# Where the pad rows of the expert queues are read from: 16 partitions with eight rows each, in place of 128 with one

## The reference

```
x = layernorm(x + dilated_attention(x))              # 16 heads, segments of 64, every second token
x = layernorm(x + cross_attention(x, ctx, ...))      # 16 heads, causal, context of 64 channels
x = layernorm(x + moe(x))                            # 32 experts, 8 for each token
```

## Time and profile before

| | us |
|---|---|
| median of three runs | 625.43 |
| lowest, highest | 625.3, 627.13 |
| span of the profiled execution | 719.4 |
| first half, until the last pad has landed (from the chain of waits) | 380.93 |
| first load of a block issued | 381.23 |
| TensorE's first work on a block | 383.46 |

### The profile page before, as it was taken

One profiled execution on the slowest core, in us unless ns is written; L12 is line 12 of the kernel. 1 busy time (PEld: TensorE's weight loads), 2 busy tenths in 40 slices (PEclk: granted clock), 3 DMA queues, 4 the chain that ended last, 5 costly groups with the idle time before them and its releaser, 6 DMA issues.

```text
span 719.4 us, 17476 instructions
## 1 busy us (share of the span) xinstructions
PE 563.9 (78%) x5097; PEld 414.4 (58%) x5098; DVE 368.4 (51%) x1527; ACT 330.1 (46%) x1204; POOL 390.5 (54%) x599
## 2 busy tenths in 40 slices
PE   3768787888878888888306889988998888985995
PEld 2445454544555554444105777777777776774884
DVE  1537566666677566666402444444444444443453
ACT  2445555455455455456003555555555554553012
POOL 5443445545544455545551666766666666665432
PEclk9789999999999899999556999999999999998899
DMA  9999996111111111112285554555555454554994
GB/s 206 277 275 365 342 339 231 69 59 73 68 50 64 55 73 73 65 66 74 99 308 182 155 165 150 160 156 167 152 164 159 143 157 142 164 160 148 425 418 145
DMA packets 83069, 121.31 MB, mean 169 GB/s; under 512 B 13779, under 2 KB 72669, under 8 KB 80992
## 3 DMA queue, kind: packets, MB, share of 16 engines
q1 hardware_dynamic: 64128, 78.46, 36.3%
q0 software_dynamic: 14016, 38.44, 14.7%
q10 hardware_dynamic: 4896, 4.03, 1.7%
HBM read 56.07 MB, written 69.01 MB: 174 GB/s over the span
## 4 chain that ended last, share of the span: by engine, by line
PE 54%; issue 12%; ACT 12%; DVE 9%; DMA 6%; ACTq 3%; POOL 2%; SPq 1%; another core or an unknown queue 0%; DVEq 0%; POOLq 0%
PE bank L793 14%; PE bank L809 9%; ACT pr L870 7%; PE bank L611 5%; PE bank L785 5%; PE bank L601 4%; PE bank L803 3%; PE bank L661 3%; DMA out<-fin 3%; PE bank L744 2%; DMA wall<-results 2%; DVE nmax L1024 2%; PE bank L619 2%; ACTq L296 1%; DVE tg L1218 1%
## 5 line engine op out<-in xcount | busy, mean ns | idle before, releaser
L556 POOL DMA_INDIRECT results<-ys,wcol x152 | 150.1, 988 | 25.8 <-POOL pscrap L545 22.0
L530 POOL DMA_INDIRECT queues<-x,xidx x128 | 129.1, 1009 | 36.9 <-issue 36.5
L793 PE MATMUL bank<-wall,xtT 128*128 x616 | 127.1, 330 | 0.7 <-issue 0.7
L870 ACT ACTIVATE pr<-bank,nmax 128x128 f32<-128x128 f32 x256 | 90.9, 370 | 29.1 <-DVE nmax L1024 29.1
L1218 DVE SCALAR_TENSOR_TENSOR tg<-th,bank 128x96 f32<-128x96 f32 x154 | 39.1, 254 | 125.3 <-ACT th L957 96.9
L793 PEld LDWEIGHTS bank<-wall,xtT 128*128 128x128 f32 x616 | 98.4, 194 | 1.4 <-issue 1.3
L963 ACT ACTIVATE ys<-bank,wcol 128x256 f32<-128x256 f32 x152 | 71.9, 473 | 54.6 <-PE bank L809 36.6
L809 PE MATMUL bank<-wall,hT 96*128 x304 | 94.5, 392 | 0.0
L785 PE MATMUL bank<-ident,xt 128*128 128x128 f32 x310 | 63.3, 286 | 35.4 <-DMA xt<-queues 24.1
L785 PEld LDWEIGHTS bank<-ident,xt 128*128 128x128 f32 x310 | 59.0, 197 | 49.9 <-DMA xt<-queues 25.1
L876 ACT COPY prT<-bank 128x512 f32<-128x512 f32 x64 | 38.5, 601 | 88.9 <-PE bank L611 86.2
(11 more groups left out here) (178 smaller groups left out, 947.2 us busy)
## 6 DMA issues: line engine op xcount, KB each, us to landing
xt<-queues SPq DMA_DIRECT2D x162, 160.0 KB
results<-zeros SPq DMA_DIRECT2D x16, 1024.0 KB
wall<-results SPq DMA_DIRECT2D x16, 1024.0 KB, 12.7
queues<-zeros SPq DMA_DIRECT2D x32, 160.0 KB, 4.9
wall<-in_L_ffn_w_gate SPq DMA_DIRECT2D x4, 768.0 KB
wall<-in_L_ffn_w_up SPq DMA_DIRECT2D x4, 768.0 KB
wall<-in_L_ffn_w_down SPq DMA_DIRECT2D x4, 768.0 KB
results<-ys,wcol POOLq DMA_INDIRECT x152
```

The costliest lines, as they stand in the source:

```text
L530: pool.indirect_dma_start(xg, bass.IndirectOffsetOnAxis(ap=xidx[:, par, k:k + 1], axis=0), x2[:, par, :], None, bounds_check=last_row, oob ...
L556: pool.indirect_dma_start(yr, bass.IndirectOffsetOnAxis(ap=wcol[:, u, 1:2], axis=0), ys[:, u, :], None, bounds_check=last_y, oob_is_err=Fa ...
L793: ins = pe.matmul(bank[2 + u % 2][:, 0:2 * INTER].rearrange("p (g i) -> p g i", g=2), xtT[:, u % 2, kk, :], wall[:, bass.ds(e, GU)].rearrange(
L870: ins = act.activation(pr[:, g % 2, q, :], pS[g % 2][:, q * P:(q + 1) * P], ACT.Exp, bias=nmax[:, 4 * g + q:4 * g + q + 1], accum_out=den[ ...
```

## The change

The pad's source is no longer `zeros` but the first 16 partitions of `xt`. GpSimd fills their eight slots with the pad row (two more memsets behind those of `zeros`), so that each of the 16 partitions holds eight pad rows one behind the other, 10,240 bytes. A pad's DMA then has 16 rows of 2560 words on both sides. Bytes, number and issuers of the pads are the same, and `zeros` stays for the idle blocks and for clearing `results`.

```diff
+PADP = P // UN
...
-N_CONST = 49
+N_CONST = 51
...
                 for r in rows:
-                    eng.dma_start(xg[bass.ds(r, P), :], zeros[:, :]).then_inc(signal, 16)
+                    eng.dma_start(xg[bass.ds(r, P), :].rearrange("(p k) w -> p (k w)", k=UN),
+                                  xt[0:PADP, :, :].rearrange("p k w -> p (k w)")).then_inc(signal, 16)
...
             def late_constants():
                 put(pool.memset, zeros[:, 0:D + NE], 0.0)
                 put(pool.memset, zeros[:, D + NE:XW].bitcast(I32), int(FAR))
+                put(pool.memset, xt[0:PADP, :, 0:D + NE], 0.0)
+                put(pool.memset, xt[0:PADP, :, D + NE:XW].bitcast(I32), int(FAR))
                 put(pool.memset, onesb[:, :], 1.0)
```

## The result

The changed kernel takes 659.71 us, the median of four runs (659.31 to 661.66), against 625.63 us for the kernel before on the same chip (625.3 to 627.13). The ratio is 1.0551, with a 95% interval of 1.0519 to 1.0583: slower by 34.1 us. The forecast was 655.5 us, range 645 to 674.

A forecast was written before the change was run, and what follows sets the result against it. Full DMA engines moving pads and scatters between the halves were taken as the bound: 49.0 us of pads plus 2.3 of scatters, 51.3 in place of 21.2, +30.1 on 625.4, gives 655.5 us, range 645 to 674.

The forecast's parts named there:

- the seam: Stretch between the halves where TensorE waits for DMA of pads and scatters; forecast to grow from 21.2 to 51.3 us.
- keep their lengths within 1 us: Sign for the profile after: first half until 358 and second half from the first block on stay as long.
- The rate: Pad reads from 16 partitions get 107 GB/s, half the `x` load's 214 on 32, so pads take 49.0 us.
- the old seam might be shorter in a run: Case of an old seam of 18.5 us in an unprofiled run: loss +32.8 us, time 658.2.
- the scatters' 2.3 us: Last batch's scatters, 1.33 MB over 128 partitions, sharing the pads' bottleneck: 1.6 to 3.1 us, taken as 2.3.
- Issue: Pad issue on SP and ScalarE and the `tab_p` reload between batches: back-pressure covered by transfers, cost nothing.
- the landing behind the last issue: Time from last pad's issue to its landing, taken as on both sides, before and after, and so falling out.
- Carrying over: The +30.1 us from the 719.4 us profile added one for one to the 625.4 us run; scaled by 0.87, +26.2.
- Tens of us: Sign for the profile after: a pad's time from DMA to landing grows to tens of us.
- A: Rival for the pads: packet length counts, partitions don't; -5.7 to -2.7 us, taken as -4, 621.4 us; chance 0.11.
- B: Rival for the pads: reads half as limited as writes, 16 partitions give 214 GB/s; +4.5 us, 630; chance 0.06.
- C: Rival for the pads: packets collide besides, 72 GB/s; +55 us, 680, half of that effect 668; chance 0.11.

The follow-up runs named there:

- before_again: The kernel before, unchanged, profiled a second time: span 623.2 us, with a run of 624.84 us.
- p32_first: Against the changed kernel, each pad read as 32 packets of 5120 bytes from partitions 0 to 31 of `xt`: ratio 1.0152 to the kernel before.
- p64_first: Against the changed kernel, each pad read as 64 packets of 2560 bytes from partitions 0 to 63 of `xt`: ratio 1.0150 to the kernel before.
- p32_step4: Against the changed kernel, each pad read as 32 packets of 5120 bytes from every fourth partition of `xt`: ratio 0.9987 to the kernel before.
- p16_step8: Against the changed kernel, pads of 16 packets of 10,240 bytes read from every eighth partition, not 0 to 15: ratio 1.0190 to the kernel before.
- p64_step2: Against the changed kernel, each pad read as 64 packets of 2560 bytes from every second partition of `xt`: ratio 0.9976 to the kernel before.
- p128_xt: Against the changed kernel, pads of 1280-byte packets from all 128 partitions of `xt`, both memsets widened to 128: ratio 0.9996 to the kernel before.
- p32_loads: Pads as in p32_step4, with both loads of the pads' places moved ahead of the first pad: ratio 0.9980 to the kernel before.

## Why the prediction was right

**The bound.** That every us of the seam is one of the end was right: 34.6 us more in the seam, 34.1 in the runs, TensorE's busy time in the two halves the same within 0.4 us (before_again). The sign that I had named, that the halves "keep their lengths within 1 us", could not be read against the first profile, which was stretched outside the seam. Against the second it holds: SP's first pad goes out at 299.3 and 299.5 us, and from the last landing to the end it is 302.6 and 302.5.

**The rate.** The step from 214 GB/s on 32 partitions to half of it on 16 was the heart, and 107 was foretold where 103 was measured, which makes 5.24 / 0.103 = 50.9 us of pads in place of 49.0. The doubt whether it holds for reads is settled by p32_first (205 GB/s reading, 214 writing). The reason given there, fewer partitions, was too coarse: p64_first has twice the partitions of p32_first and the same rate, p32_step4 has as many and nearly twice the rate. Which partitions they are decides. Halving came out right because the 16 partitions of the change are neighbours; for every eighth partition (p16_step8) it would have foretold the same loss of 30 us, and 11.9 was measured. The Trainium skill, "SBUF — State Buffer", section "Door 1: The DMA port swizzle", has it by position: a port serves two groups of four neighbouring partitions, 0 to 63 reach the same 8 of 16 ports as 0 to 31, and 0 to 15 reach 4. The runs agree where the engines are fully busy: 103 GB/s for its 4 ports, 205 and 208 for 8, 364 and 381 for 16. Its 104 GB/s was nearer than my 107. p16_step8, with 8 ports by its map, gave 208 while three queues ran, as the map has it, and 178 at a share of 0.73 over its whole window, which the map does not explain.

**The rest of the seam.** I summed 51.3 us in place of 21.2, +30.1; it was +34.6. Of the 4.5 us that are missing, 1.9 are the rate. Another 1.3 lie in the old seam: in the stretched first profile it is 377.10 + 3.83 - 358.44 = 22.5 us from first pad to last landing, in before_again 21.2, the case that the prediction named when it said that the old seam might be shorter in a run. And in the last five us the pads of ScalarE ran alone at a share of 0.67 (70 GB/s), which loses 1.6 us against 103 GB/s. These make 4.8, so nothing large is left over; the scatters' 2.3 us were not measured by themselves.

ScalarE, which has the last pads, was late twice. Its two loads of `tab_p` (here the row of the changed kernel, then that of before_again: shortest, median and longest in ns, first and last start) took 5.18 and 10.34 us in place of 2.53 and 5.13, and its first pad went out 4.4 us behind SP's in place of 1.8:

```profile
L289 ACTq TENSOR_LOAD <-tab_p x2: 5180/7758/10335, 298.4 to 332.9; - x2
```

```profile
L288 ACTq TENSOR_LOAD <-tab_p x2: 2532/3829/5126, 298.6 to 308.4; - x2
```

If that is the reason for the low share, the step "Issue", costed at nothing, was off by those 1.6 us, and so was the step that let the landing behind the last issue fall out: it took 6.21 us in place of 2.52. No run tested it in the changed kernel.

**Carrying over.** One for one was nearer than scaling the whole by 0.87: the old seam shrank from 22.5 us in the stretched profile to 21.2, by 0.94, and between the two profiles that are not stretched +34.6 us of seam are +34.1 in the runs.

**The memsets.** 2.4 us was foretold, the timeline of the changed kernel shows 2.37, and the idle time of GpSimd that covers it shrinks from 8.07 to 5.84:

```profile
20.08 2.37 POOL L407 MEMSET xt<- 16x2304 f32 x2
...
28.31 0.73 POOL L417 TENSOR_TENSOR gm<-xs,own 128x256 f32<-128x256 f32 x1
...
35.05 0.58 POOL L499 TENSOR_TENSOR rz<-ve,power 128x1 f32<-128x1 f32 x1 [5.84 <-DVE ve L1014]
```

p128_xt puts their price in the runs at nothing, -0.3 us.

**Landing.** "Tens of us" was too much. The row below is of all 32 pads of the changed kernel: 11.1 us in the median, 21.5 at most. Those of GpSimd alone have a median of 14.3, where it was 3.2 and in before_again 5.2.

```profile
DMA to landing us min/median/max: 3.4/11.1/21.5
```

**Packets and clock.** The change did what it says. The page's two hardware queues have 62560 and 3328 packets, 1568 fewer each, together 3136 where 3100 was foretold. TensorE's grant was 0.50 through the longer seam, its lower level, and its busy time in the 240 us behind it the same as in before_again.

**The rivals.** A (length counts, not partitions) has a true part only where the partitions are spread: p32_step4 and p64_step2, 381 and 364 GB/s against 341. That part is smaller than A's price of -4 us: 1.1 and 0.8 us of seam. B (16 partitions give 214 GB/s when they are read) falls with the change's own 103. C (collisions at 72 GB/s) falls with 103. The working gave most of C's chance to the range up to 674; C's own price of 680 lies above it, and only half of the effect, 668, inside.

## What to carry to other kernels

Where a stretch waits for bytes, count which partitions a transfer touches before counting its packets: 16 neighbours gave 103 GB/s, 32 or 64 neighbours 205, and 32 or 64 spread over all 128 gave 364 to 381. Long packets are worth having (12% of the rate here) if the rows are put on partitions with a step, every fourth or every second, in place of the first ones. A load elsewhere in the same trace, 214 GB/s at a full DMA share on 32 partitions, was enough to foresee a loss of 34 us within 5, since the 16 partitions were neighbours too.

## What the runs showed of the hardware

Reads of SBUF by DMA are limited by which partitions they touch: 205 GB/s from 32 neighbours, 381 from 32 spread ones with packets of the same length. A write to 32 neighbours at a time gave 214; writes to a few partitions with a step were not tried. Two queues that read from different groups of partitions at once add up to 170 GB/s on average, 1.65 times one, between 193 and 148. With 16 neighbours short packets gave 96 GB/s at a share of 0.87, long ones 103 at 0.96. A register load on ScalarE between two pads took 10.34 us with the slow pads and 4.82 us with fast ones (p32_step4); ahead of all pads, in p32_loads, two such loads took 2.09 and 2.21 us.
